# An LSTM step on one Trainium2 core: one sigmoid over two PSUM banks for cell and output factor, h kept halved

## The reference

```python
def step(carry, xw_t):            # xw_t: x @ Wx + b of this step
    prev_h, prev_c = carry
    a = xw_t + prev_h @ Wh
    i = sigmoid(a[:, :H]); f = sigmoid(a[:, H:2 * H])
    o = sigmoid(a[:, 2 * H:3 * H]); g = tanh(a[:, 3 * H:])
    next_c = f * prev_c + i * g
    next_h = o * tanh(next_c)
    return (next_h, next_c), next_h

x = x + lstm(x, cond)             # 1,024 steps, one after the other
ys = y / 16                       # y is the condition, 16 = sqrt(256)
d = rsqrt(einsum('bi,io->bo', ys * ys, weight * weight) + 1e-8)
x = x + einsum('bsi,io->bso', x * ys[:, None, :], weight) * d[:, None, :]
```

## Time and profile before

| | |
|---|---|
| median of 3 runs | 1,780.48 us (1,779.52 to 1,782.09) |
| the profiled execution's own time | 1,782.03 us |
| its span, first to last instruction | 1,780.2 us |
| mean granted clock of TensorE | 0.994 of full |
| busy: PE, PE loads, VectorE, ScalarE, GpSimd | 94%, 90%, 56%, 62%, 15% |

### The profile page before, as it was taken

One profiled execution on the slowest core, in us unless ns is written; L12 is line 12 of the kernel. 1 busy time (PEld: TensorE's weight loads), 2 busy tenths in 40 slices (PEclk: granted clock), 3 DMA queues, 4 the chain that ended last, 5 costly groups with the idle time before them and its releaser, 6 DMA issues.

```text
span 1780.2 us, 355694 instructions
## 1 busy us (share of the span) xinstructions
PE 1666.3 (94%) x164108; PEld 1608.2 (90%) x164108; DVE 1002.0 (56%) x7455; ACT 1098.2 (62%) x8196; POOL 259.4 (15%) x1293
## 2 busy tenths in 40 slices
PE   7999999999999999999999999999999999999998
PEld 6999999999999999999999999999999999999996
DVE  2555555555555555555555555555555555555554
ACT  2666666666666666666666666666666666666663
POOL 0111111111111111111111111111111111111110
PEclk7999999999999999999999999999999999999999
DMA  2000000000000000000000000000000000000001
GB/s 84 19 0 0 0 0 0 0 0 0 0 0 0 0 0 0 0 0 0 0 0 0 0 0 0 0 0 0 0 0 0 0 0 0 0 0 0 0 0 47
DMA packets 4585, 6.69 MB, mean 4 GB/s; under 512 B 1248, under 2 KB 3040, under 8 KB 4576
## 3 DMA queue, kind: packets, MB, share of 16 engines
q1 hardware_dynamic: 3872, 5.51, 0.9%
q10 hardware_dynamic: 704, 1.05, 0.2%
HBM read 4.46 MB, written 2.10 MB: 4 GB/s over the span
## 4 chain that ended last, share of the span: by engine, by line
PE 82%; DVE 12%; ACT 3%; issue 3%; DMA 0%; SPq 0%; POOL 0%; DVEq 0%
PE pG L227 35%; PE pX L209 19%; PE pH L227 14%; PE pS L227 14%; DVE pH L371 4%; DVE pH L347 4%; ACT fgate L185 3%; DVE hst L378 2%; DVE parts L366 2%; DVE pG L343 1%; PE pG L308 1%; DMA xh<-in_xT_dram 0%; PE pS L299 0%; DVE ores L395 0%; SPq L114 0%
## 5 line engine op out<-in xcount | busy, mean ns | idle before, releaser
L227 PE MATMUL pG<-hst,wh_sb 128*32 128x16 f32 x65536 | 1082.9, 187 | 98.0 <-DVE hst L378 88.0
L227 PEld LDWEIGHTS pG<-hst,wh_sb 128*32 128x32 f32 x65536 | 942.5, 109 | 148.3 <-DVE hst L378 112.8
L185 ACT ACTIVATE fgate<-pH 128x2 f32<-128x2 f32 x2048 | 354.8, 173 | 600.1 <-PE pH L227 599.8
L227 PE MATMUL pH<-hst,wh_sb 128*32 128x16 f32 x32768 | 673.5, 185 | 3.2 <-issue 3.2
L366 DVE TENSOR_TENSOR parts<-fgate,pH 128x2 f32<-128x2 f32 x2048 | 319.9, 156 | 583.1 <-ACT fgate L185 582.9
L227 PEld LDWEIGHTS pH<-hst,wh_sb 128*32 128x32 f32 x32768 | 589.2, 110 | 1.8 <-issue 1.8
L227 PE MATMUL pS<-hst,wh_sb 128*32 128x16 f32 x32768 | 506.6, 186 | 4.1 <-issue 4.1
L209 PE MATMUL pX<-xp,wx_sb 128*32 128x8 f32 x32896 | 459.4, 181 | 2.7 <-issue 1.6
L227 PEld LDWEIGHTS pS<-hst,wh_sb 128*32 128x32 f32 x32768 | 424.3, 108 | 4.3 <-issue 4.3
L146 POOL TENSOR_TENSOR xh<-xh,hst 128x4 f32 (+1 forms) x1024 | 208.7, 204 | 1491.5 <-DVE hst L378 1491.5
L371 DVE TENSOR_TENSOR_SCAN pH<-parts 128x6 f32<-128x6 f32 x2048 | 367.1, 179 | 82.7 <-ACT parts L187 0.7
(11 more groups left out here) (41 smaller groups left out, 99.8 us busy)
## 6 DMA issues: line engine op xcount, KB each, us to landing
outT_dram<-ores SPq DMA_DIRECT2D x8, 256.0 KB, 2.5
xh<-in_xT_dram SPq DMA_DIRECT2D x6, 320.0 KB
wh_sb<-in_Wh_dram ACTq DMA_DIRECT2D x1, 1024.0 KB, 8.0
wx_sb<-in_Wx_dram SPq DMA_DIRECT2D x1, 1024.0 KB, 7.5
w_sb<-in_w_dram SPq DMA_DIRECT2D x1, 256.0 KB, 7.0
xh<-in_xT_dram SPq DMA_DIRECT2D x2, 64.0 KB, 8.0
condT<-in_condT_dram ACTq DMA_DIRECT2D x1, 2.0 KB, 7.7
bias_col<-in_bC_dram ACTq DMA_DIRECT2D x1, 3.0 KB, 7.4
```

Of the source, the lines that this page charges most:

```text
L185: act.activation(fgate[:, j, :], forgets[j][:, cols], ACT.Sigmoid).then_inc(fgate_ready[j], 1)
L227: last = pe.matmul(to[c * Q:(c + 1) * Q, :], tile(wh_sb[:, k, :], c, j, g), hst[:, k, WIDE * t:WIDE * (t + 1)], start=False, stop=True, sk ...
```

## The change

- Tanh and output gate of half 0 become one sigmoid: the scan of half 0 now writes its cell into a bank of its own (bank 0 of a pS with three banks), at such columns that the cell of step t lies opposite the output sums of step t in the next bank. cell_and_out(t) is a pattern of 2 banks x 2 values.
- For that the output sums lie SCAN = 3 columns apart, in PE's writes and in the carry; the cell of half 0 is kept times 4 (the scan's unit is 4 and -2), so that its sigmoid is that of 2c.
- tanh(c) is 2 (sigmoid(2c) - 0.5): the factor 2 is left out, so h is kept halved. VectorE computes (sigmoid - 0.5) x gate with SCALAR_TENSOR_TENSOR for both halves; half 1's tanh becomes a sigmoid of scale 4.
- Wh is doubled (its g columns times 4), h0 halved. GpSimd makes h whole (h + h) in an operation of its own, waits for it and then adds it to x.
- The warm-up matmuls write into pX instead of a bank pF of their own.

```diff
-        outs = [pS[:, j, 0:WIDE] for j in range(K)]
-        tanhc = [tanh_sb[:, :], pH[:, 1, AT_LAST:AT_LAST + B]]
-        ogate = [pS[:, 0, AT_LAST:AT_LAST + B], ogate_sb[:, :]]
-        cellc = [pH[:, j, AT_CELL:AT_CELL + B * SCAN] for j in range(K)]
+        both_outs = pS[:, 1:1 + K, SCAN - 1:SCAN - 1 + SCAN * ROWS:SCAN]
+        outs = [pS[:, 1 + j, SCAN - 1:SCAN - 1 + SCAN * WIDE:SCAN] for j in range(K)]
+        tanh_1 = pH[:, 1, AT_LAST:AT_LAST + B]
+
+        def cellc(j, t):
+            return pH[:, 1, AT_CELL:AT_CELL + B * SCAN] if j else pS[:, 0, B * SCAN * t:B * SCAN * (t + 1)]
+
+        def cell_and_out(t):
+            return pS[:, 0:2, B * SCAN * t + SCAN - 1:B * SCAN * (t + 1):SCAN]
...
-                        pool.tensor_tensor(now, now, hst[:, :, at:at + B].unsqueeze(3), ALU.add).then_inc(xh_ready, 1)
+                        pool.tensor_tensor(whole[:, s, :, :], hst[:, :, at:at + B], hst[:, :, at:at + B], ALU.add).then_inc(whole_ready, 1)
+                        pool.wait_ge(whole_ready, it * T + (s + 1))
+                        pool.tensor_tensor(now, now, whole[:, s, :, :].unsqueeze(3), ALU.add).then_inc(xh_ready, 1)
...
-                    cell_tanh(0)
-                    out_gate(0).then_inc(factors_ready[0], 1)
-                    out_gate(1)
-                    cell_tanh(1).then_inc(factors_ready[1], 1)
+                    act.wait_ge(cell_ready[0], it * T + (s + 1))
+                    act.wait_ge(osum_ready[0], it * T + (s + 1))
+                    act.activation(factors_0[:, :, :], cell_and_out(s), ACT.Sigmoid).then_inc(factors_ready[0], 1)
+                    act.wait_ge(osum_ready[1], it * T + (s + 1))
+                    act.activation(ogate_1[:, :], outs[1][:, cols], ACT.Sigmoid)
+                    act.wait_ge(cell_ready[1], it * T + (s + 1))
+                    act.activation(tanh_1, cellc(1, s)[:, SCAN - 1::SCAN], ACT.Sigmoid, scale=4.0).then_inc(factors_ready[1], 1)
...
-            dve.tensor_scalar(wh_sb[:, :, g_cols], wh_sb[:, :, g_cols], 2.0, None, ALU.mult).then_inc(operands_ready, 1)
+            for of, by in ((wh_sb[:, :, g_cols], 4.0), (wh_sb[:, :, 0:G_ * D], 2.0)):
+                dve.tensor_scalar(of, of, by, None, ALU.mult).then_inc(operands_ready, 1)
...
-                        dve.tensor_tensor(hst[:, j, at:at + B], tanhc[j], ogate[j], ALU.mult).then_inc(h_ready[j], 1)
+                        cell_part, gate = ((factors_0[:, 0, :], factors_0[:, 1, :]), (tanh_1, ogate_1[:, :]))[j]
+                        dve.scalar_tensor_tensor(out=hst[:, j, at:at + B], in0=cell_part, scalar=-0.5, in1=gate,
+                                                 op0=ALU.add, op1=ALU.mult).then_inc(h_ready[j], 1)
```

More of the change, by code:

```diff
@@ L48, in build @@
         fgate = sb("fgate", [P, K, B])
-        ogate_sb = sb("ogate_sb", [P, B])
-        tanh_sb = sb("tanh_sb", [P, B])
+        factors_0 = sb("factors_0", [P, 2, B])
+        ogate_1 = sb("ogate_1", [P, B])
+        whole = sb("whole", [P, T, K, B])
         zeros = sb("zeros", [P, P])
@@ L62, in build @@
         pG = ctx.enter_context(nc.psum_tensor("pG", [P, K, 512], F32))
-        pS = ctx.enter_context(nc.psum_tensor("pS", [P, K, 512], F32))
+        pS = ctx.enter_context(nc.psum_tensor("pS", [P, 1 + K, 512], F32))
         pH = ctx.enter_context(nc.psum_tensor("pH", [P, K, 512], F32))
         pX = ctx.enter_context(nc.psum_tensor("pX", [P, 512], F32))
-        pF = ctx.enter_context(nc.psum_tensor("pF", [P, 512], F32))
         pairs = [pG[:, j, 0:2 * WIDE].rearrange("p (n r) -> p n r", r=WIDE) for j in range(K)]
@@ L69, in build @@
         cells = [[pairs[j][:, 0, :], forgets[j], pairs[j][:, 1, :]] for j in range(K)]
-        outs = [pS[:, j, 0:WIDE] for j in range(K)]
-        tanhc = [tanh_sb[:, :], pH[:, 1, AT_LAST:AT_LAST + B]]
-        ogate = [pS[:, 0, AT_LAST:AT_LAST + B], ogate_sb[:, :]]
-        cellc = [pH[:, j, AT_CELL:AT_CELL + B * SCAN] for j in range(K)]
+        both_outs = pS[:, 1:1 + K, SCAN - 1:SCAN - 1 + SCAN * ROWS:SCAN]
[5 more added lines that the diff above has]
+            return pS[:, 0:2, B * SCAN * t + SCAN - 1:B * SCAN * (t + 1):SCAN]
         xcells = [pX[:, j * NG * ROWS:(j + 1) * NG * ROWS].rearrange("p (n r) -> p n r", r=ROWS) for j in range(K)]
         xouts = pX[:, K * NG * ROWS:K * (NG + 1) * ROWS].rearrange("p (j r) -> p j r", r=ROWS)
-        pD, pO = pS[:, 0, :], [pG[:, j, :] for j in range(K)]
+        pD, pO = pS[:, 1, :], [pG[:, j, :] for j in range(K)]
         x_begun, x_loaded, cond_loaded, w_loaded, wx_loaded, wh_loaded, bias_loaded = (sem(n) for n in (
@@ L90, in build @@
         parts_ready = [sem(f"parts_ready{j}") for j in range(K)]
-        bias_doubled = sem("bias_doubled")
+        bias_doubled, whole_ready = sem("bias_doubled"), sem("whole_ready")
         pair_carried = sem("pair_carried")
@@ L239, in filler @@
                 for _ in range(count):
-                    pe.matmul(pF[0:Q, 0:P], picks[:, :], zeros[:, :], start=start, stop=True, skip_group_check=True)
+                    pe.matmul(pX[0:Q, 256:256 + P], picks[:, :], zeros[:, :], start=start, stop=True, skip_group_check=True)
             pe.wait_ge(zeros_ready, 1)
@@ L255, in _ @@
             sum_x_outs().then_inc(x_summed, 1)
-            pe.wait_ge(operands_ready, 3)
+            pe.wait_ge(operands_ready, 4)
             pe.wait_ge(outs_carried, 1)
@@ L318, in _ @@
             dve.memset(parts[:, :, :], 0.0).then_inc(buffers_zeroed, 1)
-            for j in range(K):
-                dve.memset(cellc[j], 0.0).then_inc(buffers_zeroed, 1)
+            for of in (pS[:, 0, 0:T * B * SCAN], cellc(1, 0)):
+                dve.memset(of, 0.0).then_inc(buffers_zeroed, 1)
             dve.memset(hst[:, :, :], 0.0).then_inc(buffers_zeroed, 1)
             dve.wait_ge(buffers_zeroed, 4)
-            dve.memset(parts[:, :, 1:B * SCAN:SCAN], 1.0)
-            dve.memset(parts[:, :, B * SCAN + 1::SCAN], -0.5)
+            for j, unit in enumerate((4.0, 1.0)):
+                dve.memset(parts[:, j, 1:B * SCAN:SCAN], unit)
+                dve.memset(parts[:, j, B * SCAN + 1::SCAN], -0.5 * unit)
             dve.wait_ge(cond_loaded, 16)
@@ L337, in _ @@
             dve.wait_ge(wh_loaded, 16)
[L338 removed]
+            for of, by in ((wh_sb[:, :, g_cols], 4.0), (wh_sb[:, :, 0:G_ * D], 2.0)):
+                dve.tensor_scalar(of, of, by, None, ALU.mult).then_inc(operands_ready, 1)
             for j in range(K):
[L340 removed]
+                dve.tensor_scalar(hst[:, j, h_slot(0):h_slot(0) + B], condT[:, j, :], 0.5, None, ALU.mult).then_inc(h_ready[j], 1)
             def carry_pair(j):
@@ L350, in carry_outs @@
             def carry_outs():
-                dve.tensor_tensor(pS[:, :, 0:ROWS], xouts, bias_o[:, :].unsqueeze(2).broadcast_to([P, K, ROWS]),
+                dve.tensor_tensor(both_outs, xouts, bias_o[:, :].unsqueeze(2).broadcast_to([P, K, ROWS]),
                                   ALU.add).then_inc(outs_carried, 1)
@@ L365, in _ @@
                         dve.wait_ge(fgate_ready[j], it * T + (s + 1))
-                        dve.tensor_tensor(parts[:, j, (B + 1) * SCAN - 1::SCAN], fgate[:, j, :], cellc[j][:, SCAN - 1::SCAN],
+                        dve.tensor_tensor(parts[:, j, (B + 1) * SCAN - 1::SCAN], fgate[:, j, :], cellc(j, (s - 1) % T)[:, SCAN - 1::SCAN],
                                           ALU.mult).then_inc(parts_ready[j], 1)
@@ L370, in _ @@
                         dve.wait_ge(parts_ready[j], it * (2 * T) + 2 * (s + 1))
-                        dve.tensor_tensor_scan(cellc[j], parts[:, j, 0:B * SCAN], parts[:, j, B * SCAN:2 * B * SCAN], 0.0,
+                        dve.tensor_tensor_scan(cellc(j, s), parts[:, j, 0:B * SCAN], parts[:, j, B * SCAN:2 * B * SCAN], 0.0,
                                                ALU.mult, ALU.add).then_inc(cell_ready[j], 1)
```

## The result

The changed kernel takes 1,864.43 us (median of 4, 1,863.65 to 1,867.0), the kernel before 1,780.15 beside it: **4.7% slower**, ratio 1.0474 with a 95% interval of 1.0456 to 1.0492. The prediction was 1,884 with a range of 1,805 to 1,945. The difference is 84.3 us, 0.082 for each of the 1,024 steps. One of the eleven executions of experiment 3's kernel, 2,791 us against 1,780 to 1,782 for the others, is left out of its ratio.

What follows compares the result with a forecast made beforehand. Half 0's chain, not TensorE's total, was taken to bound the kernel. Sigmoid 0.020, wait 0.07 and product 0.01 made +0.10 us a step, +102 over 1,024 steps; plus 1, less 1.6: 1,884 us, range 1,805 to 1,945.

Steps and rivals of the forecast that it cites:

- The chain through half 0: Half 0's h to forget gate (0.80 us), TensorE's groups, output gate 0, product: claimed to set the 1.69 us step.
- The separate wait: Ahead of the joint sigmoid, the wait on osum_ready[0], written last, becomes its own instruction: +0.07 us a step.
- rival of a harmless wait: The wait made its own instruction is the cell's, through before the sum: +0.03 us a step, 1,812 us; chance 0.12.
- The sigmoid: Joint sigmoid on ScalarE writes four values to SBUF, 177 ns against output gate 0's 157: +0.020 us a step.
- The product: VectorE's half 0 product as (a - 0.5) x b, both inputs from SBUF: +0.01 us, bounds 0 and +0.08.
- Stride: TensorE writing output sums three columns apart in PSUM: 0 taken, other bound +0.05 us on the chain.
- the rival at 1,939: The 16 records of strided output sum 0 go at the slow-clock pace: +0.05 us a step, 1,939 us; chance 0.10.
- GpSimd: Adding h to x in two operations delays what follows by at most 0.44 us, covered by idle time: 0.
- Start-up and end: One more VectorE pass over Wh and one more GpSimd operation before the last layer: 1 us together.
- The clock: Rival: longer TensorE pauses drop the granted clock to 1.2 GHz, 0.3 us a step, above 2,190 us; chance 0.02.
- Half 1's slack: Half 1's h reaching the forget gate, read from one step near 122 us: at least 0.07 us of slack.
- rival of a faster kernel at 1,720: ScalarE's queue, not TensorE, holds output gate 0, so dropping tanh gives -0.06 us a step, 1,720 us; chance 0.04.

Runs made afterwards that it cites:

- experiment 3: The kernel before with the products of h as SCALAR_TENSOR_TENSOR ((tanh x 1.0) x gate), operands where they were: 1,780.96 us, ratio 1.0003.
- experiment 2: The kernel before with one more, already satisfied wait for cell_ready[0] ahead of output gate 0, osum_ready[0] written last: 1,843.71 us, ratio 1.0352.
- experiment 1: The changed kernel with the two waits ahead of the joint sigmoid exchanged, osum_ready[0] first and cell_ready[0] last: 1,807.82 us, ratio 1.0154.
- experiment 4: The kernel before with output gate 0 written to SBUF instead of PSUM: 1,803.71 us, ratio 1.0133.
- experiment 5: The kernel before with the sums of all gates of both halves three columns apart in PSUM: 1,780.33 us, ratio 1.0002.
- experiment 6: The kernel before without the first-half part of output sum 0 (8 of 16 matmul records left out, h wrong): 1,777.75 us, ratio 0.9985.
- experiment 7: The changed kernel with one semaphore for cell and output sum of half 0, and 8 of 16 records of output sum 0 left out: 1,778.53 us, ratio 0.9994.
- experiment 8: The changed kernel, waits exchanged, with output sum 0, joint sigmoid and half 0's product moved ahead of half 1's last sums, parts and scan: 2,010.07 us.

## Why the prediction was right, and where it was not

**The chain through half 0** was right: TensorE's part stayed at 0.80 to 0.81 and every term on the link from osum_ready[0] to h showed up in the step.

**The separate wait** was the main term and has the right sign, place and nearly the right size: +0.07 forecast from VectorE's row, 0.061 alone in experiment 2. The order of the lines told which wait it would be, and exchanging them gave 57 us back. Its rival of a harmless wait, forecast at 1,812, is what experiment 1 built, at 1,808.

**The sigmoid**, +0.020 from L187's 177 ns, was 0.017: the group measured 174. Nearly all of it is the destination and not the four values (experiment 4). **The product**, +0.01, was 0.004. Of the two things that I named, the form is free (experiment 3), and the gate in SBUF is not (experiment 4). The upper bound of 0.08 from the 128x512 row was far off. These three terms, 0.082 instead of 0.10, are nearly all of the 20 us by which 1,884 is high.

**Stride** at 0 was right; the rival at 1,939 (its 0.05 a step, as rounded, would be 51 us and 1,935) falls by experiment 5, where all sums were strided and none got slower. **GpSimd** at 0 was right: its second operation starts 0.38 behind the first (903.15, 903.53), the copy for the next x sums ends at 902.13, and TensorE begins them at 902.28. The danger named beside it, a scan of cell 0 made longer by GpSimd, came true in six steps only: the scan takes 0.48 to 0.50 there and the step 1.93 to 1.95. That is 1 us in all, and the kernel before had 0.7 of it. **Start-up and end**, 1 us allowed: from the first h of half 0 to the last it is 1,746.6 us in the profiled execution before (14.38 to 1,761.02) and 1,831.2 after (14.84 to 1,846.08), so the span outside the loop grew from 33.6 to 34.0. The first h alone comes at 14.40 to 14.76 in experiments 2, 3 and 4, whose start-up is that of the kernel before, so 0.4 tells little. **The clock** did not fall: the mean granted clock is 0.994 as before, the upper level of 2.4 GHz from the second of the 40 slices on, and that rival falls.

**Half 1's slack** was the step that failed. I read from the step at 122 that half 1 had at least 0.07 us of slack. That step shows only that nothing is won when half 1 comes earlier; how late it may come it doesn't show. No step of the kernel before shows that, for half 1 is never more than 0.27 behind half 0 there. It took runs in which half 1 came late: in experiments 6, 7 and 8 the gate is never less than 0.53 to 0.54 behind it, and 0.54 is where the kernel before stands. Half 1 had no slack at all. That the forecast was not touched is luck: the change made half 0 later and so loosened half 1. The rival of a faster kernel at 1,720 rested on that slack: it could not have come true even with TensorE out of the way, for half 1 would have kept the step at 1.69 (1,778 in experiment 7).

## What to carry to other kernels

Count the waits ahead of each operation on a chain. Where two stand, write first the one that is satisfied last, or let both producers increment one semaphore; here that decided 57 of 84 us. Merging two operations saves nothing where the engine that runs them is waiting for another, and the merged one brings the destination and the waits of both. Before counting on a gain in one of two chains that close through the same gate, find for each the shortest distance at which it has released the gate, in a step or a run in which the other was early. A chain has slack only as far as its distance now is longer than that.

## What the runs showed of the hardware

- Of two waits ahead of an operation the one written last is an instruction of its own, on VectorE and on ScalarE (L198 in the changed kernel and in experiment 1, L196 in experiment 2). It costs ScalarE 0.061 us when it is satisfied last (experiment 2), and nothing measurable when it is through early (1.0154 against 1.0145 without it).
- ScalarE's output gate 0 takes 157 ns to PSUM and 172 to SBUF, and four values to SBUF take 174 (factors) to 177 (parts). The 157 hold where it waits for TensorE: started 0.06 behind tanh 0 it takes 170 (experiment 6).
- VectorE's product of half 0 takes 157 with the gate from PSUM and 161 with both inputs from SBUF. Half 1's, with tanh from PSUM and the gate from SBUF, takes 160, as a plain product before and with a constant after.
- fp32 matmuls of 16 columns write PSUM with a step of three columns at full pace (1.0002, interval 0.9992 to 1.0011).
- A VectorE scan of 0.18 us takes 0.30 to 0.31 in the kernel before, 0.48 to 0.50 in the changed one and 0.51 to 0.55 in experiment 1 where a GpSimd operation of 128x256 (0.61 us) runs beside it, in six steps of each.
